# Reordering the first slots of a two-block transformer kernel: early Exp table, constant products, norms and flips of pairs 1 to 3 spread over three slots

## The reference, cut to what matters

```python
x = x + attn(_layernorm(x))          # eight layers, below
x = x + experts(_layernorm(x))       # top 2 of 8 experts, not touched by the change

def layer(h):                        # 16 heads of 8
    q = elu(h @ wq + bq) + 1; k = elu(h @ wk + bk) + 1; v = h @ wv + bv
    kv = einsum('bshd,bshm->bhdm', k, v)
    z = 1 / (einsum('bshd,bhd->bsh', q, k.sum(1)) + 1e-6)
    h = _ln(h + att(q, kv, z) @ wo + bo)
    return _ln(h + gelu(h @ w1 + c1) @ w2 + c2)
```

## Time and profile before

| | |
|---|---|
| median of three runs | 1065.08 us (1064.76 to 1065.31) |
| profiled execution | 1067.03 us |
| its span, first to last instruction | 1065.3 us |
| mean granted TensorE clock | 0.976 |
| busy share PE / DVE / ACT / POOL | 94% / 78% / 78% / 72% |
| first projection of layer 0 begins | 16.34 us |

### The profile page before, as it was taken

How to read it: one execution, slowest core, us unless ns; L and a number is a source line. 1 busy time by engine, 2 the same in 40 slices (tenths; PEclk the granted TensorE clock), 3 DMA queues, 4 the chain that set the end, 5 groups by cost and what they waited for, 6 DMA issues and landing times.

```text
span 1065.3 us, 25018 instructions
## 1 busy us (share of the span) xinstructions
PE 997.0 (94%) x7558; PEld 932.4 (88%) x7558; DVE 830.9 (78%) x2733; ACT 831.4 (78%) x1621; POOL 770.0 (72%) x1157
## 2 busy tenths in 40 slices
PE   5899999999999999999999999999998859989993
PEld 4799989999999999989999999899997759889993
DVE  6777887888888878887888788787889888953545
ACT  5878887888888888888888888888887645765582
POOL 5866877787877778777777777777766677677753
PEclk9999999999999999999999999999999878999997
DMA  4101263136314432443144315501302345667363
GB/s 140 51 1 36 55 130 60 36 75 111 59 38 96 90 59 42 99 90 60 40 100 100 63 42 122 95 8 21 100 1 80 93 130 162 178 190 219 102 182 129
DMA packets 196371, 92.81 MB, mean 87 GB/s; under 512 B 119788, under 2 KB 179187, under 8 KB 196112
## 3 DMA queue, kind: packets, MB, share of 16 engines
q1 hardware_dynamic: 190352, 81.71, 32.9%
q0 software_dynamic: 4544, 8.47, 2.3%
q10 hardware_dynamic: 1344, 1.05, 0.3%
HBM read 42.98 MB, written 31.54 MB: 70 GB/s over the span
## 4 chain that ended last, share of the span: by engine, by line
PE 72%; POOL 6%; DVE 6%; issue 5%; DMA 4%; SPq 4%; ACT 2%; DVEq 0%; POOLq 0%; ACTq 0%
PE psum L1943 19%; PE psum L1820 8%; PE psum L1822 8%; PE psum L1821 8%; PE psum L1867 6%; PE psum L1901 5%; PE psum L1873 5%; PE psum L1855 4%; PE psum L2102 4%; POOL xs L929 4%; PE psum L2086 4%; SPq L508 3%; DMA this_w<-w 2%; DVE stat L1240 1%; PE psum L1964 1%
## 5 line engine op out<-in xcount | busy, mean ns | idle before, releaser
L1026 ACT ACTIVATE s<-s,shift,rstd 128x128 f32<-128x128 f32 x496 | 203.9, 485 | 40.7 <-POOL shift L761 40.3
L1943 PE MATMUL psum<-this_w,hid 128*128 128x128 f32 x1792 | 216.5, 277 | 3.0 <-DMA this_w<-w 3.0
L1943 PEld LDWEIGHTS psum<-this_w,hid 128*128 128x128 f32 x1792 | 208.5, 193 | 4.2 <-DMA this_w<-w 4.2
L1005 ACT ACTIVATE hid<-psum,col 128x512 f32<-128x512 f32 x256 | 155.2, 683 | 2.3 <-PE psum L1822 1.7
L759 POOL TENSOR_TENSOR rstd<-var,neg_half 128x4 f32<-128x4 f32 x132 | 146.3, 1108 | 11.0
L802 POOL TENSOR_TENSOR res_a<-s,row 128x512 f32<-128x512 f32 x60 | 77.4, 1290 | 73.6 <-ACT s L1026 68.4
L1240 DVE BATCH_NORM_STATS2 stat<-s 128x6 f32<-128x128 f32 x512 | 110.0, 277 | 0.0
L756 POOL TENSOR_SCALAR shift<-mv 128x4 f32<-128x4 f32 x132 | 25.8, 195 | 100.1 <-DVE mv L1244 98.8
L1820 PE MATMUL psum<-x_hi,this_w 128*128 128x512 f32 x224 | 95.5, 426 | 1.2 <-DVE x_lo L1312 1.2
L787 POOL TENSOR_TENSOR res_f<-res_f,row 128x512 f32<-128x512 f32 x64 | 92.3, 1443 | 5.0
L2102 PE MATMUL psum<-heads,hid 128*128 x624 | 86.7, 284 | 6.8 <-ACT hid L1158 5.6
(11 more groups left out here) (270 smaller groups left out, 2761.3 us busy)
## 6 DMA issues: line engine op xcount, KB each, us to landing
xs<-pad SPq DMA_DIRECT2D x18, 975.0 KB, 8.8
feature<-xrow SPq DMA_DIRECT2D x416, 32.0 KB, 2.0
res_a<-w SPq DMA_DIRECT2D x28, 256.0 KB
xblk<-xs SPq DMA_DIRECT2D x78, 65.0 KB
row<-rows SPq DMA_DIRECT2D x8, 512.0 KB, 5.4
raw_w<-w SPq DMA_DIRECT2D x15, 256.0 KB, 3.0
this_w<-next_w SPq DMA_DIRECT2D x7, 512.0 KB, 3.2
this_qkv<-next_qkv SPq DMA_DIRECT2D x6, 384.0 KB, 2.9
```

The source lines that it names most:

```text
L1005: a.activation(hid[h][:, c, :], ps(3 + h + c), ACT.Gelu, bias=col[:, bass.ds(lw * FF + (C_C1 + c), 1)]).then_inc(hid_done, 1)
L1026: ins = a.activation(dst[:, t, :], src[:, t, :], ACT.Identity, bias=shift[i][:, t:t + 1], scale=rstd[i][:, t:t + 1])
L1943: ins = t_.matmul(ps(down_bank(l, s, h))[:, t * P:(t + 1) * P], hid[h][:, c, t * P:(t + 1) * P], down[:, c, :], start=c == 0, stop=c == FF ...
```

## The change

The change reorders the lists of all five engines around the first slots. It touches layer 0 and what comes ahead of it.

- ScalarE runs one Exp on a constant as its first instruction, and half 0's norm comes ahead of the copy that rounds the projection weights.
- TensorE runs 16 products of a constant 128x128 tile of ones as its first instructions, into a bank that nobody reads. The flip of half 0, the bias products (now in bank 6 rather than 1) and the projection of half 0 follow, then the flip and the projection of half 1.
- The first norm writes into `res_a`, where `start_resid` adds the bias row in place, after the half's flip. The Gelu's wait for all eight residuals goes away.
- Half 2 is normed ahead of slot 0, halves 3 to 5 in slot 0, halves 6 and 7 in slot 2 (their moments and scales in slot 1). Flips: 2 and 3 in slot 0, 4 and 5 in slot 1, 6 and 7 in slot 2. High and low parts and residuals move along. Each flip of halves 4 to 7 waits for a Gelu of its bank.
- GpSimd takes the first weight split ahead of the scales of halves 3 to 5. Two semaphores of late loads are joined into one, and one is renamed. The order of SyncE's DMAs is the same.

```diff
 # shared
         def first_norm(u):
-            return hid[u % 2][:, u // 2, :].rearrange("p (t n) -> p t n", t=T)
+            return res_a[:, u]
-        START_BANK = (4, 5, 6, 7, 6, 7, 4, 5)
+        START_BANK = (4, 5, 6, 7, 4, 5, 4, 5)
+        def bias_bank(l):
+            return 1 if l else 6
...
 # gpsimd
                 pool.wait_ge(x2_done, u + 1)
-                g.tensor_tensor(res_a[:, u], first_norm(u), rows_of(R_BIN, 0), ALU.add).then_inc(resa_done, 1)
+                pool.wait_ge(t2_mm, u + 1)
+                g.tensor_tensor(res_a[:, u], first_norm(u), rows_of(R_BIN, 0), ALU.add).then_inc(first_resid, 1)
...
             start(2)
-            start(3)
             scale_w1(0)
-            for u in range(4, HALVES):
-                start(u)
             hi_w1(0)
             lo_w1(0)
+            start(3)
+            start(4)
             sum_rows(0, 0)
             wait(pool, rows_summed, 8)
-            for u in range(HALVES // 2):
-                start_resid(u)
+            start_resid(0)
+            start_resid(1)
+            start(5)
...
-                    if first and s == 1:
-                        for u in range(HALVES // 2, HALVES):
-                            start_resid(u)
                     resid_f(l, s - 1, 0)
                     resid_f(l, s - 1, 1)
+                    if first:
+                        start_resid(2 * s)
+                        start_resid(2 * s + 1)
+                    if first and s == 1:
+                        start(6)
+                        start(7)
...
 # scalar
-                if l == 0:
-                    wait(act, resa_done, HALVES)
...
+            act.wait_ge(const_step, 7)
+            a.activation(warm[:, 0:1], ones[:, 0:1], ACT.Exp).then_inc(exp_table, 1)
+            start(0)
             act.wait_ge(raw_in, 32)
             a.activation(this_qkv[:, 0, :], raw_qkv[:, :], ACT.Copy).then_inc(qkv_split, 4)
-            start(0)
+            start_split(0)
             start(1)
-            start_split(0)
             start_split(1)
             start(2)
-            start(3)
...
                     start_split(2)
-                    start_split(3)
-                    for u in range(4, HALVES):
-                        start(u)
-                    start_split(4)
-                    start_split(5)
+                    start(3)
+                    start(4)
+                if first and s == 2:
+                    start(6)
                 if p1:
                     load_table(ACT.Gelu, 0, gelu_table, l * SLOTS + (s - 1))
                     split_x1(l, s - 1, 1)
                     gelu(l, s - 1, 0)
+                if first and s == 2:
+                    start(7)
...
+                if first and 1 <= s < 3:
+                    start_split(2 * s + 2)
+                    start_split(2 * s + 3)
...
                 if first and s == 0:
-                    start_split(6)
-                    start_split(7)
+                    start_split(3)
+                    start(5)
...
 # vector
+            start_lo(0)
             start(2)
-            start(3)
-            start_lo(0)
+            biases(0, 0)
             start_lo(1)
-            biases(0, 0)
-            start(4)
-            start(5)
-            start(6)
...
-                if first and s == 0:
-                    start(7)
...
                 if first and s == 0:
+                    start(3)
                     start_lo(2)
-                    start_lo(3)
...
                 mask_kv(l, s, 1)
+                if first and s == 0:
+                    start(4)
                 attend(l, s, 0)
                 attend(l, s, 1)
...
                 if first and s == 0:
-                    start_lo(4)
-                    start_lo(5)
+                    start_lo(3)
+                    start(5)
+                if first and s == 1:
+                    start(6)
+                    start(7)
...
+                if first and 1 <= s < 3:
+                    start_lo(2 * s + 2)
+                    start_lo(2 * s + 3)
                 if p1:
                     add_res2(l, s - 1, 0)
                 add_res1(l, s, 0)
...
 # tensor
-                    wait(pe, xt_lo_done, (2 if s == 0 else HALVES) if first and s < 3 else banks_upto(l, s - 3))
+                    wait(pe, xt_lo_done, 2 * s + 2 if first else banks_upto(l, s - 3))
...
+                if u == 2:
+                    pe.wait_ge(bias_done, 8)
+                elif u >= 4:
+                    pe.wait_ge(hid_done, upto(0, u // 2 - 2, 1, per=FF) - 3 + u % 2)
+                flip(START_BANK[u], first_norm(u)).then_inc(t2_mm, 1)
+            def keep_clock(n):
+                for _ in range(n):
+                    t_.matmul(ps(3)[:, 0:P], ones[:, :], ones[:, :], start=True, stop=True)
+            pe.wait_ge(const_step, 7)
+            keep_clock(16)
             pe.wait_ge(const_done, 1)
...
             start(0)
+            bias_products(0)
+            project(0, 0, 0, True, False)
             start(1)
-            bias_products(0)
+            project(0, 0, 1, True, False)
...
                 attention(l, s, 1, first)
+                if first and s == 0:
+                    start(3)
                 if p1:
                     ff_up(l, s - 1, 1)
-                if first and s == 0:
-                    start(4)
-                    start(5)
                 flip_att(l, s, 0)
+                if first and 1 <= s < 3:
+                    start(2 * s + 2)
...
                 if p1:
                     ff_down(l, s - 1, 0)
+                if first and 1 <= s < 3:
+                    start(2 * s + 3)
                 if first and s == 0:
-                    pe.wait_ge(xt_lo_done, 6)
+                    pe.wait_ge(xt_lo_done, 4)
                 out_proj(l, s, 0)
                 out_proj(l, s, 1)
-                if first and s == 0:
-                    start(6)
-                    start(7)
```

More of the change, by code:

```diff
@@ L131, in resid_upto @@
     l, p = ORDER[l * SLOTS + s]
-    return HALVES + (2 * ORDER.index((l - 1, p)) + h + 1 if l else 2 * p + h + 1 - HALVES)
+    return 2 * ORDER.index((l - 1, p)) + h + 1 if l else 2 * p + h + 1
 def flips_upto(i, h):
@@ L373, in build @@
         x_in = [sem(f"x_in{u}") for u in range(HALVES)]
-        col_in, row_in, router_in = sem("col_in"), sem("row_in"), sem("router_in")
+        col_in, row_in, late_in = sem("col_in"), sem("row_in"), sem("late_in")
         raw_in, last_in = sem("raw_in"), sem("last_in")
@@ L402, in build @@
         resf_mul, resf_done, resa_mul, resa_done = (sem(n) for n in ("resf_mul", "resf_done", "resa_mul", "resa_done"))
-        offset_done, mv0_done, std0_done, outer_done, bef_in = (
-            sem(n) for n in ("offset_done", "mv0_done", "std0_done", "outer_done", "bef_in"))
+        offset_done, mv0_done, std0_done, outer_done, first_resid = (
+            sem(n) for n in ("offset_done", "mv0_done", "std0_done", "outer_done", "first_resid"))
         p_step, mvg_done, std_done, fin_ready = (sem(n) for n in ("p_step", "mvg_done", "std_done", "fin_ready"))
@@ L493, in _ @@
                 sp.dma_start(x_all[:, u], x[u]).then_inc(x_in[u], 16)
-            sp.dma_start(r_raw[:, :], router).then_inc(router_in, 16)
-            sp.dma_start(bef[:, :], rows[LAYERS, R_B1 * P:(R_B1 + 1) * P].partition_broadcast(P)).then_inc(bef_in, 16)
+            sp.dma_start(r_raw[:, :], router).then_inc(late_in, 16)
+            sp.dma_start(bef[:, :], rows[LAYERS, R_B1 * P:(R_B1 + 1) * P].partition_broadcast(P)).then_inc(late_in, 16)
             set_wo(0)
@@ L811, in prep_router @@
             def prep_router():
-                pool.wait_ge(router_in, 16)
+                pool.wait_ge(late_in, 32)
                 g.tensor_scalar(r_sc[:, :], r_raw[:, :], col[:, C_GAMMA:C_GAMMA + 1], 0.0, ALU.mult, ALU.add).then_inc(r_prep, 1)
@@ L1112, in slot @@
                     norm2(l, s - 2, 1)
-                load_table(ACT.Exp, 1, exp_table, l * SLOTS + s)
+                load_table(ACT.Exp, 1, exp_table, l * SLOTS + s + 1)
                 if flips:
@@ L1297, in add_res1 @@
                 wait(dve, wo_mm, upto(l, s, h))
-                wait(dve, resa_done, resid_upto(l, s, h))
+                wait(dve, resa_done if layer_at(l, s) else first_resid, resid_upto(l, s, h))
                 wait(dve, t1_mm, upto(l, s - 1, h))
@@ L1356, in biases @@
                 wait(dve, row_in, l * 16 + 16)
-                b = ps(1)
+                b = ps(bias_bank(l))
                 kvb = row[:, ring, R_BK:R_BK + 2, :]
@@ L1410, in stack_moments @@
                 if u < T:
-                    wait(dve, resa_done, HALVES + 2 * ORDER.index((LAST, u // 2)) + u % 2 + 1)
+                    wait(dve, resa_done, 2 * ORDER.index((LAST, u // 2)) + u % 2 + 1)
                 half_moments(0, u, res_a, mv0_done)
@@ L1836, in project @@
                 if h == 1:
-                    wait(pe, xt_lo_done, (2 if s == 0 else HALVES) if first and s < 3 else banks_upto(l, s - 3))
```

(11 more changed lines are left out.)

10 lines of the change are left out of this document (2 added, 8 removed).

## The result

The change made the kernel slower: 1074.3 us (median of four runs, 1073.8 to 1075.43) against 1064.92 for the kernel before on the same chip, a ratio of 1.0086 (interval 1.0064 to 1.0109). A second measurement on another occasion gave 1071.08 against 1065.7, 1.0053 (1.0035 to 1.0072). The direction was forecast; the first median lies 2.1 us above the range, the second inside it.

A forecast was written before the change was run, and what follows sets the result against it. TensorE was taken as the bound from slot 1's attention (50.13 us), a chain over four engines before it. Losses 5.4 minus gain 3.25 gave 2.2; clock 1.6 made 3.8, on 1065.08: 1068.9 us, range 1067.2 to 1071.

The forecast's parts named there:

- The start: Ahead of slot 1's attention: first projection at 10.4, second at 14.6, attention at 46.9 instead of 50.13, gaining 3.25 us.
- The first rival: Start stays at the low clock level: first projection 12.2, second 18 to 19, time 1069.3 to 1071.1; chance 0.12.
- The losses in full slots: Behind slot 1's attention: flips, late norms and waits moved into full slots lose 5.4 us in all.
- four flips: Slots 1 and 2: two flips moved into each cost TensorE 0.44 apiece, 1.76 us.
- late low part of half 5, slot 2's norms: Slot 1, VectorE: low part waits for a flip, residual adds queue behind, slot 2's norms come 0.4 us later.
- half 6's norm ahead of the table load: Slot 2, ScalarE: norm of 1.54 against some 0.3 of slack delays table load and split, losing 1.3 us.
- half 6's flip behind a Gelu: Slot 2: flip waits for a Gelu that half 7's norm has pushed back, 0.3 us.
- slot 3's query step: Slot 3: half 7's split waits for a flip; feed-forward input's flip comes 0.9 us late.
- GpSimd and the second norms, next slot: Slot 3: two new input residuals on GpSimd delay second norms and Gelu; next slot starts 0.8 us later.
- Flips are free: Flips fit beside TensorE's weight loads, or clock never falls in slots 0 and 1: 1067.1 to 1067.3, both 1065.5; chance 0.20.
- The clock's share: Slots 0 and 1: thin TensorE work brings one low clock stretch on slot 1's projections, 1.6 us (bounds 0 to 3.9).
- something that could swallow the loss: Layer 1: TensorE's weight-load wait absorbs the net 2.2, giving 1065.1, or 1063.3 without slow products; chance 0.10.

The follow-up runs named there:

- the relaid order: Changed kernel with its new start kept, norms moved where nothing TensorE waits for stands behind them, splits, low parts and residuals moved along; 1065.78 us, ratio 0.9998.
- the second profile: Changed kernel run once more with no edit; 1071.08 us.

## Why the prediction was right and where it was wrong

**The start.** Right, each step 0.2 to 0.3 late: first projection 10.74 for 10.4, second 14.93 for 14.6, slot 1's attention 47.07 for 46.9. Gain at the gauge, the start of slot 1's attention, 3.06 for 3.25. The first rival, a start at the low level, falls with it. Of the 5.6 at the first projection the rest was eaten by norms on ScalarE, as worked out: exchanging two steps alone moved slot 1's first flip by 1.88, and the relaid order brought slot 1 to 43.65 to 44.17.

**The losses in full slots.** Right in mechanism; too small in sum. The measured column has the waits of the first profile, and for the flips what four more of them cost.

| term | forecast | measured |
|---|---|---|
| four flips | 1.76 | 1.76 (flips twice: 0.87 and 0.89) |
| late low part of half 5, slot 2's norms | 0.4 | 0.34 |
| half 6's norm ahead of the table load | 1.3 | 1.37 |
| half 6's flip behind a Gelu | 0.3 | 0.58 |
| slot 3's query step | 0.9 | 0.65 |
| GpSimd and the second norms, next slot | 0.8 | 1.43 |

The measured terms make 6.13, the table of attentions 6.49, the forecast 5.4. The 0.36 between the first two has no wait over 0.3 us to its name. The term most off is the last, for GpSimd's two input residuals of 1.36 each and the second norm and Gelu behind them: 0.8 where 1.43 was waited. No run tested this cause, or those of the 0.34 and the 0.65, by itself; of the waits only the 1.37 had a run of its own.

**Flips are free** (the second rival) is refuted. The Trainium skill's page ("Perfetto Trace Analysis", Identifying the Most-Contended Engine) sends the reader to the share of the peak that the products reach (MFU) and the weight loads' share for the room that is left. No run here shows such room for a flip: with a share of 4.43 of 5 flips cost their full time. The rival's other half, a clock that never falls in slots 0 and 1, did not come either (low from 39.9 to 43.3).

**The clock's share.** 1.6 was taken for one stretch. It is not one number: the same program paid nearly nothing for it in one execution (from slot 1's first norm to its attention 8.98, for 8.94 taken from before) and 1.84 more in the next. So it is in part luck that layer 0's 3.43 lies near the 3.8 forecast: the losses were 1.1 larger, the gain 0.2 smaller, and the clock's 1.6 did not come.

**The step that failed** is the last of the sum: "The sum: 2.2 + 1.6 = 3.8 us" was put on the median of before as if everything behind layer 0 stayed as it was, so the waits for the weight load entered it at nothing. Layer 0 did cost 3.43 and 5.27. But in the first profile the load's waits, 5.2 instead of 3.0 us, and to a small part the 0.3 in layer 6 put another 1.96 on it up to the last layer, and routing and experts 1.1. The prediction knew this wait, but only in layer 1 and only as something that could swallow the loss. It goes both ways: layer 1 gave back 1.4 in the second profile and 2.6 with doubled flips, and layer 3 took 2.2 in the first profile. A range whose upper end stood on layer 0's clock alone was too narrow by these. With the waits gone from both kernels the medians are 4.9 apart, against the 3.8 forecast and the 9.4 and 5.4 measured with them.

What stays open is the 2.6 of the 9.4 that lie between the medians and the executions profiled; no trace shows them. The second median, 1071.08, lies inside the range, so how far the first was missed is in part a matter of the occasion.

Open: what sets the length of routing and experts. From the last layer's last attention to the end thirteen profiles have 245.5 to 248.9 us, and one, of the kernel before with the early load, 252.8. Before has 246.2 and after 247.3 and 247.8; whether the 1.1 and 1.6 between them belong to the change was not settled.

## What to carry to other kernels

Work that fills a wait at the start is gained only up to the next engine list that it lengthens: ask what stands behind each moved step on its own engine, and put it where nothing on the path does. In slots where the bound engine never waits, every added instruction counts in full, and a moved wait turns up a slot later. Before an edit of some microseconds is judged, remove the waits that vary from run to run (here one DMA issued five places earlier), for they hide it or double it.

## What the runs showed of the hardware

The granted clock fell at different places in executions of the same program, 39.9 to 43.3 us in one and 30.3 to 37.1 in the next, the one right behind a wait of TensorE of 2.48 us, the other within one of 2.33. Products of a constant that nobody reads, put into these waits, kept the level high from 8 us to the end of layer 0 in the one profile taken, and cost nothing that the time shows.

A load of 256 KB issued ahead of four block DMAs and a row load instead of behind them (148.82 instead of 151.11 us, in a run that was itself 1.0 behind) landed in 2.9 to 3.8 us instead of 5.3 to 7.8 and took all of its waits away: 3.0 us in the kernel before, whose median fell by as much.
